# Reordering short vector and scalar steps between the tiles of an attention pass

## The reference

```python
h = tok(x)                                   # token layer, linear attention-like memory
z = layernorm(h)
# attention with a group weight
scores = (q @ k.T) * scale
gw     = softmax(gelu(v @ W_gp));  G = gw @ gw.T
w      = (1 - a) * softmax(scores * G) + a * G
h      = h + (w @ v) @ W_proj + b_proj
x2     = layernorm(h)
# soft mixture of 64 experts with 16 slots each
phi_n  = phi * rsqrt(sum(phi**2, axis=0) + 1e-6)   # sum over the 64 experts, per slot and feature
logits = x2 @ phi_n                                # 1024 columns
Xs = softmax_over_tokens(logits).T @ x2;  Ys = experts(layernorm(Xs))
h  = h + softmax_over_slots(logits) @ Ys
```

## Time and profile before

| what | value |
|---|---|
| median of 3 runs | 441.89 us (441.79 to 443.79) |
| the profiled execution, its own time | 441.72 us |
| its span in the trace | 439.9 us |
| PE busy | 416.6 us, 95% of the span |
| DVE busy | 309.6 us, 70% |
| ACT busy | 233.6 us, 53% |
| POOL busy | 147.6 us, 34% |

### The profile page before, as it was taken

How to read it: one execution, slowest core, us unless ns; L and a number is a source line. 1 busy time by engine, 2 the same in 40 slices (tenths; PEclk the granted TensorE clock), 3 DMA queues, 4 the chain that set the end, 5 groups by cost and what they waited for, 6 DMA issues and landing times.

```text
span 439.9 us, 8403 instructions
## 1 busy us (share of the span) xinstructions
PE 416.6 (95%) x3106; PEld 348.1 (79%) x3106; DVE 309.6 (70%) x776; ACT 233.6 (53%) x426; POOL 147.6 (34%) x243
## 2 busy tenths in 40 slices
PE   8899999999996899899999899999999799999995
PEld 6577766888896798788889888899956578778895
DVE  6799864877777788678988987777675335344464
ACT  5678735898443466644225758988854221212220
POOL 5885201773304732200002960023722222121310
PEclk9999999999998999999999999999999999999999
DMA  3126102001000000000000050009179999999305
GB/s 101 60 75 228 61 2 78 31 2 31 1 1 0 0 1 0 3 0 1 0 1 3 0 215 1 1 2 371 59 295 417 366 354 373 390 371 374 141 11 144
DMA packets 14232, 50.24 MB, mean 114 GB/s; under 512 B 3504, under 2 KB 8240, under 8 KB 9968
## 3 DMA queue, kind: packets, MB, share of 16 engines
q1 hardware_dynamic: 7584, 43.21, 26.1%
q0 software_dynamic: 2912, 3.96, 3.0%
q10 hardware_dynamic: 3696, 2.54, 1.9%
HBM read 46.53 MB, written 3.15 MB: 113 GB/s over the span
## 4 chain that ended last, share of the span: by engine, by line
PE 73%; DMA 11%; DVE 6%; POOL 4%; ACT 3%; issue 2%; SPq 0%; POOLq 0%; ACTq 0%; DVEq 0%
DMA w1r<-in_p_w 10%; PE ps L1035 8%; PE ps L1198 6%; PE ps L972 4%; PE ps L951 3%; PE ps L1139 3%; PE ps L976 3%; PE ps L1168 2%; PE ps L740 2%; PE ps L641 2%; PE ps L1015 2%; PE ps L1016 2%; PE ps L1017 2%; PE ps L1018 2%; PE ps L1019 2%
## 5 line engine op out<-in xcount | busy, mean ns | idle before, releaser
L1198 PE MATMUL ps<-ys,ct 128*128 128x192 f32 x256 | 45.2, 330 | 1.2 <-DMA ys<-ys_dram 1.2
L2038 DVE TENSOR_TENSOR res<-ps,res 128x384 f32<-128x384 f32 x64 | 35.7, 558 | 14.7 <-PE ps L1198 10.2
L1198 PEld LDWEIGHTS ps<-ys,ct 128*128 128x128 f32 x256 | 41.2, 190 | 4.6 <-issue 2.7
L520 POOL TENSOR_SCALAR ve<-mv 128x1 f32<-128x1 f32 x32 | 12.9, 402 | 89.6 <-DVE mv L1877 59.8
L629 POOL DMA_DIRECT2D ys<-ys_dram x32 | 19.6, 618 | 69.0 <-DMA ys_dram<-ysb 67.8
L1421 ACT CAST et<-ps 128x512 fp32r<-128x512 f32 x32 | 17.3, 590 | 41.5 <-PE ps L951 41.5
L1537 ACT ACTIVATE hs<-ps 128x384 f32<-128x384 f32 x16 | 7.9, 491 | 57.7 <-PE ps L1139 57.7
L2029 DVE COPY ysb<-ps 128x192 f32<-128x192 f32 x16 | 5.7, 357 | 38.8 <-PE ps L1168 38.8
L1413 ACT ACTIVATE zz<-zz,nmx 128x1024 f32<-128x1024 f32 x16 | 18.4, 1152 | 19.5 <-DVE nmx L1853 19.5
L1860 DVE TENSOR_TENSOR etl<-ps,et 128x512 fp32r<-128x512 f32 x32 | 20.7, 686 | 10.0 <-ACT et L1421 9.9
L1892 DVE CUSTOM_DVE_ANT_0 ec<-ps,zero 128x1024 f32<-128x1024 f32 x16 | 19.5, 1221 | 9.2 <-PE ps L1019 9.2
(11 more groups left out here) (311 smaller groups left out, 1223.7 us busy)
## 6 DMA issues: line engine op xcount, KB each, us to landing
w1r<-in_p_w SPq DMA_DIRECT2D x16, 1152.0 KB, 19.1
w2r<-in_p_w SPq DMA_DIRECT2D x16, 1152.0 KB, 18.9
ys_dram<-ysb ACTq DMA_DIRECT2D x16, 96.0 KB, 8.8
ys<-ys_dram POOLq DMA_DIRECT2D x32, 48.0 KB, 7.2
phT<-in_p_phi SPq DMA_DIRECT2D x1, 1024.0 KB, 4.7
wT<-in_p_qkv SPq DMA_DIRECT2D x1, 774.0 KB, 4.4
out<-res SPq DMA_DIRECT2D x3, 192.0 KB, 3.4
out<-res ACTq DMA_DIRECT2D x3, 192.0 KB, 3.9
```

The lines of the kernel that those rows point to most:

```text
L1198: last = mm(bank(5 + q % 3)[:, h * D:(h + 1) * D], ct[:, u % 2, k + h, :], ys[:, t % YR, b, :], start=True, stop=True)
L2038: v.tensor_tensor(res[:, i:i + 2, :], bank(5 + q % 3)[:, 0:2 * D].rearrange("p (h d) -> p h d", h=2), res[:, i:i + 2, :], ALU.add).then_in ...
```

## The change

Four things are reordered, and one instruction is cut in two.

1. The low parts of the second sequence's gates (`gw_lo(2)`, `gw_lo(3)`) are taken at the end of stages 2 and 3, in front of `beside`, where they stood at the start of stages 3 and 4, behind it.
2. The sum of phi's squares is taken in two halves, one in stage 1 and one in stage 2; GpSimd waits for both.
3. `values_lo(1)`, the two scalings of phi and its two low parts each move one stage later on VectorE; the two high parts of phi move one stage later on ScalarE.
4. In stage 8 ScalarE takes the high parts of x2 tiles 0 and 1 ahead of the tiles 2 and 3, and VectorE takes the low parts of x2 tiles 0 and 1 ahead of `beside(8)`, which now holds phi's last low part.

```diff
@@ gpsimd
-            pool.wait_ge(m["ph_summed"], 1)
+            pool.wait_ge(m["ph_summed"], 2)
@@ scalar, phi_parts
-                if s in (5, 6):
-                    act.wait_ge(m["ph_scaled"], s - 4)
-                    sc.copy(phAh[:] if s == 5 else phB[:], phT[:, s - 5, :]).then_inc(m["ph_hi"], 1)
+                if s in (6, 7):
+                    act.wait_ge(m["ph_scaled"], s - 5)
+                    sc.copy(phAh[:] if s == 6 else phB[:], phT[:, s - 6, :]).then_inc(m["ph_hi"], 1)
@@ scalar, the loop over stages
+                if s == FIRST_PASS - 1:
+                    x2_hi(0)
+                    x2_hi(1)
                 if FIRST_PASS - 1 <= s < FIRST_PASS + KT // PER_PASS - 2:
                     x2_tile(2 * (s - FIRST_PASS + 2))
                     x2_tile(2 * (s - FIRST_PASS + 2) + 1)
-                if s == FIRST_PASS - 1:
-                    x2_hi(0)
-                    x2_hi(1)
@@ vector, beside
-                if s == 2:
+                if s in (1, 2):
+                    h = s - 1
                     dve.wait_ge(m["ph_squared"], 1)
-                    v.tensor_reduce(pss[:], phsq.rearrange("d c (n p) -> d c p n", p=NP), AX, ALU.add
+                    v.tensor_reduce(pss[:, h, :], phsq[:, h, :].rearrange("d (n p) -> d p n", p=NP), AX, ALU.add
                                     ).then_inc(m["ph_summed"], 1)
-                if s == 3:
+                if s == 4:
                     values_lo(1)
-                if s in (4, 5):
+                if s in (5, 6):
...
-                if s == 6:
+                if s == 7:
...
-                if s == 7:
+                if s == 8:
@@ vector, the loop over stages
-                if 3 <= s < 3 + GTS:
-                    gw_lo(s - 1)
...
-                beside(s)
+                if 2 <= s < 2 + GTS:
+                    gw_lo(s)
                 if s == FIRST_PASS - 1:
                     x2_lo(0)
                     x2_lo(1)
+                beside(s)
```

More of the change, by code:

```diff
@@ L1819, in beside @@
             def beside(s):
-                if s == 2:
+                if s in (1, 2):
+                    h = s - 1
                     dve.wait_ge(m["ph_squared"], 1)
-                    v.tensor_reduce(pss[:], phsq.rearrange("d c (n p) -> d c p n", p=NP), AX, ALU.add
+                    v.tensor_reduce(pss[:, h, :], phsq[:, h, :].rearrange("d (n p) -> d p n", p=NP), AX, ALU.add
                                     ).then_inc(m["ph_summed"], 1)
-                if s == 3:
+                if s == 4:
                     values_lo(1)
-                if s in (4, 5):
+                if s in (5, 6):
                     dve.wait_ge(m["ph_rsqrt"], 1)
-                    h = s - 4
+                    h = s - 5
                     w = phT[:, h, :].rearrange("d (n p) -> d n p", p=NP)
                     v.tensor_tensor(w, w, bc(prs[:, h, :].unsqueeze(1), [P, NE, NP]), ALU.mult).then_inc(m["ph_scaled"], 1)
-                if s == 6:
+                if s == 7:
                     dve.wait_ge(m["ph_hi"], 1)
                     v.tensor_tensor(phAl[:], phT[:, 0, :], f(phAh[:]), ALU.subtract)
-                if s == 7:
+                if s == 8:
                     dve.wait_ge(m["ph_hi"], 2)
```

## The result

The changed kernel takes 435.19 us (median of 6 runs, 434.16 to 436.10), the kernel before 442.54 us in the same comparison (6 runs, 441.79 to 443.79). The ratio is 0.9829, 95% interval 0.9812 to 0.9845: 1.7% faster. The profiled execution has a span of 433.3 us, 6.6 less than before's 439.9.

What follows compares the result with a forecast made beforehand. TensorE works nearly all the time, so only its pauses and slow stretches can be won back; 3.36 + 2.33 + 1.13 = 6.82 us off the 439.9 span gives 433.1, as run median 435.1 us, range 434.0 to 437.4.

Steps and rivals of the forecast that it cites:

- the three stages: Attention pass, stages 2, 3 and 8: gains of 3.36, 2.33 and 1.13 us, together 6.82 us.
- Stage 2: First gate: gw_lo(2) ahead of the sum lets turn(2) start at 135.30 instead of 138.66, gain 3.36 us.
- Half sum: VectorE, stage 1: half the sum of squares takes 1.84 us, in idle time before u_take(1), costing nothing.
- Stage 3: Second gate: turn(3) at 142.96 with a pause of 0.42 left; 7.66 us long instead of 9.99, gain 2.33.
- Slow clock: Behind TensorE's longest pause, clock 0.56 goes to 1.00; rival that it stays: 1.56 us back, 436.7 us, 7%.
- cross-check: Stage 3: 9.99 - 7.24 = 2.75 us is the pause of 1.19 and 1.56 for the slow clock.
- Stages 4 to 7: Moved values_lo(1), scalings and phi parts fit idle time or replace equally long pieces: cost nothing.
- Stage 8: Earlier x2 high and low parts bring the turn 7.23 us behind the last instead of 8.36, gain 1.13.
- Transfer to the end: Weights' stream is requested by TensorE events, so all of it moves up, transfers starting about 6.8 us earlier.
- the lost-gain rival: Weights arrive at a pace set before the attention pass ends, so the gain is lost: 441.9 us, 5%.
- The dear half sums: Rival: a half sum is hardly shorter than the whole; at 3.53 us each 438.2 us, 11%.
- the slower case: Rival: the two half sums lose more than 6.8 us; at 7 us each 445.1 us, 2%.

Runs made afterwards that it cites:

- the halves alone: Kernel before with only the sum of phi's squares cut in two halves, the gates' low parts staying behind it: 439.99 us, ratio 0.9936.
- the filled pause: Kernel before with unused identity products on TensorE in the pause before turn(2): 26 products 445.07 us, ratio 1.0049; 12 products 441.88 us, ratio 0.9992.

## Why the prediction was right

The forecast was 435.1 us and the result is 435.19. The mechanism was right, and part of the closeness is luck: the three stages gave 7.08 us and not 6.82, and the stream took back 0.6 in the profiled execution. Between the medians the change is 7.35 us, against the 6.8 that was forecast: the kernel before has a median of 442.54 over six runs, where the prediction started from 441.89. Step by step:

- **Stage 2**: turn(2) 6.85 behind turn(1), worked out as 6.90. The 0.11 of pause had been the allowance of 0.10 for a signal; the high part ends at 134.27 (ScalarE) and the low part starts at 134.31.
- **Half sum**: 1.86 and 1.91 us against 1.84, so the fixed part read from two subtractions held for another operation to 0.07. The Trainium skill's rule (page "VectorE: DVE Perf Modes", section "The TRN2 errata") would have given 1.22, and the rows decide against it. The prediction overlooked a row that tells more: the kernel before has another TENSOR_REDUCE of 1024 elements, a maximum over elements that lie side by side (L1997, `colm`, read from the product banks), and it takes 1.22 us; a sum of 512 elements side by side outside them (L1658) takes 0.67. So it is not the operation that is dear. The sum over phi steps over 16 elements from one to the next; that this step is the cause fits, but no run here tests it.
- **Stage 3**: 7.48 against 7.66. Right mechanism, one term too large. I let the whole 0.2 us by which the turned tile's low parts are late run on to `finish`. They did start late, 1.61 behind the turn instead of 1.38, but `z_tile` waits for ScalarE's scores in the usual stage: it starts 1.44 behind the low parts in stage 2 (131.11 - 129.67) and 1.24 in stage 3 (137.99 - 136.75). That slack took the delay. `turn(3)` still hangs on the gate, though the view shows no idle time: the low part ends at 141.82 + 0.66 = 142.48 and the turn starts 0.14 behind it, as before, where TensorE alone would have started at 142.20 + 0.23 = 142.43 (0.23 is the step from the last L919 to a turn that does not wait). The wait that is left is 0.19 us, worked out as 0.42.
- **Slow clock**: 1.00 over the whole stretch, and the halves alone and the filled pause show that the idle pause made it. The prediction's cross-check put it at 1.56 us, which is 0.19 too much (1.37 against the filled pause): a turn that waits also loses the 0.16 by which one that does not wait starts before the last product ends. The sum did not need this term. Nor is it a constant: 2.6 us in another execution.
- **Stages 4 to 7**: 26.51 us before and after. All moved pieces were covered, as costed at nothing.
- **Stage 8**: 7.20 against 7.23, confirmed on its own (7.21; ratio 0.9974).
- **Transfer to the end**: requests 7.2 us earlier, to the tenth, so the lost-gain rival is out.
- The dear half sums and the slower case fall with the two rows of L1824.

## What to carry to other kernels

Where a buffer is shared, look at what stands in front of the instruction that frees it on its engine, not at how long that instruction is: two subtractions of 0.7 us held TensorE for 4.5 us, because 3.5 and 1.7 us of work that nobody was waiting for yet stood before them. Put the awaited piece first, and cut the unawaited one into parts that fit the idle time of separate stages, with an idle row for each part. A long pause of TensorE had a second price here, in the clock that follows it (1.4 to 2.6 us behind 3.3 us), and shortening the pause to half, 1.6 us, removed it whole.

## What the runs showed of the hardware

- A sum over elements 16 apart took 3.53 us for 2048 elements and 1.83 to 1.91 for 1024; a maximum over 1024 elements side by side took 1.22, a sum of 512 side by side 0.67.
- The granted clock stayed at 1.00 behind pauses of 0.70, 1.2, 1.36, 1.60 and 1.72 us, and was at 0.50 behind both observed pauses of 3.3 us. In both it fell while TensorE still stood idle (mean 0.94 over 135.20 to 138.60 in one, 0.65 over 137 to 138 in the other). How long it stayed there differed between the two executions with the same pause: until some 141.6 us in one and 144.1 us in the other, by windows of 1 us.
- A VectorE subtraction of 1024 elements, both inputs outside the product banks, took 2.25 us instead of 1.17 when GpSimd ran the same kind of subtraction beside it; GpSimd's two took 5.71 instead of 4.71. In the changed kernel `values_lo(1)` took 1.96 instead of 1.73 and GpSimd's copy beside it 2.03 instead of 0.61; with the sum undivided it was 2.00 and 2.03, with stage 8 alone changed 1.76 and 2.02. Moving an instruction on VectorE can so change its length by what it then stands beside; here it did not reach TensorE.
- A product of two fp32 tiles of the identity is two passes of 0.11 us in the trace (52 records in 5.96 us for 26 products), a transpose of the same size one (8 records in 1.03 us for eight).
